# A graph layer with three branches: maxima moved into attention, GpSimd splits, added rows in two transfers, identity turns on TensorE

## The reference, cut to what matters

```
xn = layernorm(x)
# graph branch (gat_conv twice, 4 heads of 192, then 2 heads of 96)
h = (layernorm(xn) * g + b) @ W;  e = leaky_relu(s_src[src] + s_dst[dst], 0.2)
alpha = softmax of e over the edges of each dst;  out = segment_sum(alpha * h[src], dst)
gnn = concat(xn, out2) @ Wu + bu
# mixing branch: random features of k and q, y = (qp @ kptv) / (D + eps), projected
x = x + gnn + mix
# experts: router softmax over 8, top 2, balanced gates, silu(f @ w1) @ w2
x = x + sum over the two chosen of gate * expert(layernorm(x))
```

## Time and profile before

| | us |
|---|---|
| median of 3 runs | 1066.67 |
| lowest, highest | 1063.98, 1069.22 |
| the profiled execution: time | 1061.51 |
| its span | 1059.8 |
| PE busy | 925.7 (87%) |
| DVE busy | 627.1 (59%) |
| ACT busy | 386.2 (36%) |
| POOL busy | 389.6 (37%) |

### The profile page before, as it was taken

One profiled execution on the slowest core, in us unless ns is written; L12 is line 12 of the kernel. 1 busy time (PEld: TensorE's weight loads), 2 busy tenths in 40 slices (PEclk: granted clock), 3 DMA queues, 4 the chain that ended last, 5 costly groups with the idle time before them and its releaser, 6 DMA issues.

```text
span 1059.8 us, 13855 instructions
## 1 busy us (share of the span) xinstructions
PE 925.7 (87%) x5064; PEld 785.8 (74%) x5064; DVE 627.1 (59%) x1222; ACT 386.2 (36%) x575; POOL 389.6 (37%) x302
## 2 busy tenths in 40 slices
PE   3899899999999999999189999897888469999993
PEld 3798785786678899999088988886877457666672
DVE  7676995602078132386989999695996763222221
ACT  2543330223344000244576766346863401121120
POOL 3058888888888874000110000000000313434441
PEclk9999999969999999999589999989988759999997
DMA  9994579333226449600140000216005924666664
GB/s 315 232 161 83 96 203 263 51 45 45 1 1 145 63 92 287 200 2 1 51 149 23 1 1 1 88 63 208 2 1 199 363 60 91 119 120 119 120 120 60
DMA packets 78417, 112.43 MB, mean 106 GB/s; under 512 B 34994, under 2 KB 53933, under 8 KB 78351
## 3 DMA queue, kind: packets, MB, share of 16 engines
q0 software_dynamic: 35264, 39.86, 22.9%
q1 hardware_dynamic: 40781, 65.39, 19.2%
q10 hardware_dynamic: 2306, 6.29, 1.5%
HBM read 80.02 MB, written 31.49 MB: 105 GB/s over the span
## 4 chain that ended last, share of the span: by engine, by line
PE 53%; DVE 20%; DMA 16%; issue 6%; ACT 2%; SPq 1%; POOL 0%; POOLq 0%; DVEq 0%; ACTq 0%
PE bank L1621 41%; DMA out<-orow,send 14%; PE bank L1890 9%; DVE pbuf L1399 4%; DVE pbuf L1373 3%; DVE sb_before L1318 3%; DVE junk_k L1194 2%; PE bank L1632 2%; DVE h L1382 2%; DMA keyrow<-key_d 2%; SPq L552 1%; DVE o L1382 1%; PE bank L1826 0%; DVE sb_stats L1142 0%; DVE xnT_lo L1118 0%
## 5 line engine op out<-in xcount | busy, mean ns | idle before, releaser
L661 POOL DMA_INDIRECT table<-match_n,slot_ix x168 | 276.2, 1644 | 90.2 <-issue 48.9
L1890 PE MATMUL bank<-h,pbuf 128*128 128x197 f32 (+1 forms) x1200 | 194.5, 324 | 29.6 <-DVE pbuf L1399 28.6
L1890 PEld LDWEIGHTS bank<-h,pbuf 128*128 128x128 f32 x1200 | 186.7, 199 | 37.4 <-DVE pbuf L1399 34.2
L1194 DVE SCALAR_TENSOR_TENSOR junk_k<-keyrow,key,sb_before 128x384 uint8<-128x384 f32 x168 | 92.7, 614 | 21.8 <-DMA keyrow<-key_d 11.5
L1318 DVE CUSTOM_DVE_ANT_0 sb_before<-a_row,pen 128x1280 bf16<-128x1280 f32 x60 | 89.4, 1491 | 27.3 <-ACT pen L958 11.2
L1606 DVE TENSOR_SCALAR orow<-bank,gates 128x384 f32<-128x384 f32 x54 | 33.4, 618 | 115.8 <-PE bank L1621 115.8
L692 POOL IOTA cst_i<- 128x128 int32 x1 | 0.2, 229 | 271.8 <-DVE o L1382 271.8
L1016 ACT ACTIVATE pbuf<-pbuf 128x1280 f32<-128x1280 f32 x60 | 76.1, 1269 | 64.4 <-DVE pbuf L1373 64.4
L1399 DVE SCALAR_TENSOR_TENSOR pbuf<-pbuf,cnt 128x1280 f32<-128x1280 f32 x60 | 88.7, 1485 | 0.0
L1621 PE MATMUL bank<-xnT_hi,w_hi 128*128 128x512 f32 (+1 forms) x216 | 85.1, 394 | 3.7 <-DVE xnT_lo L1118 2.8
L728 POOL DMA_INDIRECT out<-orow,send x27 | 42.9, 1587 | 111.5 <-DMA out<-orow,send 92.5
(11 more groups left out here) (346 smaller groups left out, 1668.4 us busy)
## 6 DMA issues: line engine op xcount, KB each, us to landing
keyrow<-key_d SPq DMA_DIRECT2D x28, 384.0 KB
cnt<-table POOLq DMA_DIRECT2D x20, 320.0 KB, 9.3
f_all<-in_w1T SPq DMA_DIRECT2D x8, 768.0 KB, 10.6
f_all<-in_w2T SPq DMA_DIRECT2D x8, 768.0 KB, 12.2
u_row<-m_d POOLq DMA_DIRECT2D x8, 640.0 KB, 6.3
w_raw<-in_kqvT SPq DMA_DIRECT2D x4, 1152.0 KB
acc_d<-ubuf SPq DMA_DIRECT2D x20, 192.0 KB, 2.6
x<-acc_d SPq DMA_DIRECT2D x10, 384.0 KB, 6.1
```

What stands on the lines that cost most here:

```text
L661: pool.indirect_dma_start(table[i], bass.IndirectOffsetOnAxis(ap=slot_ix[:, g:g + 1], axis=0), match_n[:, g:g + 1], None, compute_op=ALU.a ...
L1194: nc.vector.scalar_tensor_tensor(out=junk_k[g % 2][:, :], in0=keyrow[c % KR][:, w:w + KW * P], scalar=key[:, g:g + 1], in1=before[:, first ...
L1890: ins = nc.tensor.matmul(b[:, d * stride:d * stride + v.shape[-1]], score[:, dt * P:(dt + 1) * P], v, start=st == 0 and d == 0, stop=st == ...
```

## The change

Six edits. (1) Masks come in pairs in the second half (`PEN_AT`), the maxima are taken for heads 0 and 1 together, then head 2; those of head 3 for tiles 4 to 9 are taken inside first attention, after steps 2, 5, ... 17, and its row is written by SP straight from `ucol` in 4-byte pieces. The joining of the biases is done after step 1. The row loads of head 0 wait for the maxima of head 2. (2) The subtraction on `cnt` is spread over the last projection tiles. (3) The low part of the last weight half and the low part of the output weight (`wuo_lo`) are made by GpSimd. (4) In the middle `wuT` and `rsum` go ahead of `aR`; ScalarE starts the second attention after head 0's maxima and copies the `uR2` banks of head 1 at steps 2 and 3. (5) Each addition of result rows is two transfers of 384 channels, with a semaphore for each half. (6) TensorE turns the identity 40 times ahead of the first sums and 28 times ahead of the first expert tile.

```
-        PEN_AT = [(0, 2), (0, 4), (0, 7), (0, 8), (1, 0), (1, 1), (1, 2), (1, 3), (1, 4), (1, 5)]
-        ROWS_AT = {(1, 6): 0, (1, 9): 1}
+        PEN_AT = {(0, 2): [0], (0, 3): [1], (0, 4): [2], (0, 6): [3], (1, 0): [4, 5], (1, 1): [6, 7], (1, 2): [8, 9]}
+        ROWS_AT = {(1, 5): 0, (1, 6): 1, (1, 8): 2}
+        LESS_AT = {(1, 3): [0], (1, 4): [1, 2], (1, 5): [3], (1, 6): [4, 5], (1, 7): [6], (1, 8): [7, 8], (1, 9): [9]}
...
+            sp.wait_ge(m_done, H1)
+            sp.dma_start(m_d[2 * (H1 - 1) * NT:2 * H1 * NT, :].rearrange("(k t) p -> p k t", k=2), ucol[:, H1 - 1, :, :],
+                         allow_slow_non_contiguous=True).then_inc(m_out[H1 - 1], 16)
...
+            pool.wait_ge(w_hi_done, SPLITS.index(A0 + 1) + 1)
+            finished(pool, "wb", 1)
+            i, gain = SLOT[A0 + 1], gb_c[:, 0, :].unsqueeze(2).broadcast_to([P, KD, HALF])
+            nc.gpsimd.tensor_tensor(w_raw[i][:, :, :], w_raw[i][:, :, :], gain, ALU.mult).then_inc(gain_done, 1)
+            pool.wait_ge(gain_done, 1)
+            ins = nc.gpsimd.tensor_tensor(w_lo[i][:, :, :], w_raw[i][:, :, :], w_hi[i][:, :, :].bitcast(F32), ALU.subtract)
+            ins.then_inc(w_split, 1)
...
+            pool.wait_ge(g_hi_done, 1)
+            nc.gpsimd.tensor_tensor(wuo_lo[:, :, :], wuo_raw[:, :, :], wuo_hi[:, :, :].bitcast(F32), ALU.subtract).then_inc(g_split, 1)
...
-            def send_rows(a):
+            def send_rows(a, hf):
...
+                    pool.wait_ge(added_out[hf], 16 * a)
+                pool.wait_ge(orow_done, 2 * a + hf + 1)
+                pool.indirect_dma_start(half_rows, bass.IndirectOffsetOnAxis(ap=send[:, hf, a:a + 1], axis=0),
+                                        orow[a % 3][:, hf * HALF:(hf + 1) * HALF], None,
+                                        compute_op=ALU.add, bounds_check=2 * N - 1).then_inc(added_out[hf], 16)
...
-            act.wait_ge(max_done, MAX1 + 2 * NT)
-            attention(H1, H2, u2_row_b, row_ready_2)
+            act.wait_ge(max_done, MAX1 + NT)
+            def rows_between(i):
+                if i in (2, 3):
+                    rows_out("uR2", (i - 2,), 1, (u1_row_b, u2_row_b)[i - 2][1])
...
+            for dt in range(4, NT):
+                evacuated(dve, "pen", dt, 0), evacuated(dve, "pen", dt, 1)
+                masked_max(pen[dt], a_row, (0, 1), dt)
+            dve.wait_ge(max_done, NT)
+            leaky_max(H1, 0, 1), leaky_max(H1, 1, 1)
+            for dt in range(4, NT):
+                if dt == 7:
+                    max_row_out(0), max_row_out(1)
+                masked_max(pen[dt], a_row, (2,), dt)
+            dve.wait_ge(max_done, NT + NT - 4)
+            leaky_max(H1, 2, 1)
+            def between_first(i):
+                if i == 0:
+                    max_row_out(2)
+                if i == 1:
+                    bias_of_layer()
+                if i % 3 == 2 and i < 18:
+                    masked_max(pen[4 + i // 3], a_row, (3,), 4 + i // 3)
+                if i == 18:
+                    dve.wait_ge(max_done, MAX1)
+                    leaky_max(H1, 3, 1)
...
+            def keep_running(name, n):
+                b = take(pe, *name)
+                for _ in range(n):
+                    nc.tensor.transpose(b[:, 0:P], ident[:, :], ident[:, :])
+            keep_running(("agg", 0, 0), 40)
...
+            keep_running(("yT", 0, 0), 28)
             turn_rows(0)
```

More of the change, by code:

```diff
@@ L1016, in attention @@
                     nc.scalar.activation(pbuf[i % 3][:, :], pbuf[i % 3][:, :], ACT.Exp).then_inc(e_done, 1)
-            attention(0, H1, u2_row, row_ready_1)
-            for h in range(H2):
-                rows_out("aR", (), h, a2_row[h])
+                    between(i)
+            attention(0, H1, u2_row, row_ready_1, lambda i: None)
             act.wait_ge(g_in, 16)
@@ L1029, in _ @@
                                          ACT.Copy).then_inc(free("wuT", k, m), 1)
+            nc.scalar.activation(lr[:, NT, :], finished(act, "rsum")[:, 0:EM], ACT.Copy).then_inc(free("rsum"), 1)
+            for h in range(H2):
+                rows_out("aR", (), h, a2_row[h])
             b = finished(act, "wuR")
@@ L1351, in _, with between_second, attention @@
                 nc.vector.tensor_copy(mrow[h % 2][:, :], b[0:2 * NT, 0:P]).then_inc(free("mT", h), 1)
-            def attention(h0, heads, row_ready, u1_r, stride, chans, out_rows, added, stage, nbank, per):
+            for dt in range(4, NT):
[19 more added lines that the diff above has]
+                    leaky_max(H1, 3, 1)
+            def between_second(i):
+                pass
+            def attention(h0, heads, row_ready, u1_r, stride, chans, out_rows, added, stage, nbank, per, between):
                 seq = [(h, st) for h in range(heads) for st in range(NT)]
@@ L1812, in score_columns, with spread_row @@
                 ins.then_inc(full("dot"), 1)
+            def spread_row(stage, k, h, cols):
+                for c, (s, w) in enumerate(CHUNKS):
+                    b = take(pe, stage, *k, h, c)
+                    for t in chunk_tiles(c):
+                        ins = mm(b[:, t * P - s:(t + 1) * P - s], cols[:, t:t + 1].broadcast_to([P, P]), ident[:, :], True, True)
+                    ins.then_inc(full(stage, *k, h, c), 1)
             def max_rows(h):
@@ L1913, in _ @@
             pe.wait_ge(router_in, 16)
+            pe.wait_ge(mean_done, 2)
+            b = take(pe, "rsum")
+            for m in range(KD):
+                ins = mm(b[:, 0:EM], ones[:, :], rw_raw[:, m, :], m == 0, m == KD - 1)
+            ins.then_inc(full("rsum"), 1)
+            pe.wait_ge(dots_done, 2)
+            for h in range(H2):
+                spread_row("aR", (), h, scol[:, h, :])
             evacuated_all(pe, "wuT")
-            pe.wait_ge(mean_done, 2)
             b = take(pe, "wuR")
@@ L1920, in _ @@
             ins.then_inc(full("wuR"), 1)
-            b = take(pe, "rsum")
-            for m in range(KD):
-                ins = mm(b[:, 0:EM], ones[:, :], rw_raw[:, m, :], m == 0, m == KD - 1)
-            ins.then_inc(full("rsum"), 1)
             def spread_shifts(h):
```

133 lines of the change are left out of this document (57 added, 76 removed).

## The result

The changed kernel takes 1037.42 us (median of 4 runs, 1033.1 to 1039.45); the kernel before on the same chip takes 1067.14 (median of 4, 1063.98 to 1069.22). The ratio is 0.9719, 95% interval 0.9679 to 0.9758. On a second chip it was 1036.49 against 1063.83, ratio 0.9735 (0.9705 to 0.9764). The prediction was 1036, range 1027 to 1049.

What follows compares the result with a forecast made beforehand. It took the first gap, first attention, the middle and the experts' chain of adding transfers as what bounds the kernel. Terms summed to -30.7 us: 1061.51 to 1030.8, or 1036 on the median's scale, range 1027 to 1049.

Steps and rivals of the forecast that it cites:

- First gap: Masked maxima to first sum of attention: first sum at 518.5 instead of 534.46, -15.9 us, GpSimd passes charged to VectorE.
- the spread of head 0: Middle: TensorE there at about 705, small group done at 707.2, then 16.2 us of TensorE work to the last spread.
- Forty turns: Ahead of attention's first sums: keep TensorE's clock up; half of the 2.3 us effect credited, -1.2 us.
- What attention pays: First attention: maxima, bias additions, row copy and small group inserted on VectorE lengthen it, +6.9 us (bounds 3 and 11.9).
- Middle: Between the attentions: earlier row copies and maxima, ScalarE starting sooner; first sum at 729.8 against 738.77, -9.0 us.
- Attention 2: Second attention: first two steps at 2.5 us each, -1.8 us; six copies returning at steps 2 and 3, +0.8 us.
- Experts: Expert part: 28 turns -2.4, half-row transfers -4.4 and -3.7 us.
- the first (sends stay the bound): Experts: half lands no sooner, or GpSimd needs 6.6 us a tile; yields about 2 instead of 10.5, 1044.5; chance 0.2.
- The second (no lock): Gap and middle: maxima not locked or passes cheap; gap 2 us better, middle 3, 1031; chance 0.13.
- The fourth: Experts: the two adding transfers run one after the other; slower, 1189 at a period of 12; chance 0.04.
- The fifth: Both sets of turns: they do not do what is said, nothing else fails; 1039.5; chance 0.05.
- the third: Lock worse than charged: 5.9 us passes, TensorE waiting, clock not held, insertions near full price; 1045; chance 0.14.

Runs made afterwards that it cites:

- first profile: Profiled execution of the changed kernel in its first measurement, against the kernel before: 1039.45 us in that execution; median 1037.42 us, ratio 0.9719.
- e0: The changed kernel again, nothing altered, beside the kernel before on a second chip: 1036.49 us, ratio 0.9735.
- e1: Changed kernel with one adding transfer of a whole row per expert tile again, halves undone: 1043.75 us, ratio 0.9818.
- e3b: Repeat on another chip of the changed kernel with both low splits back on VectorE: 1024.57 us, ratio 0.9646.
- e3: Changed kernel with both low splits moved from GpSimd back to VectorE: 1024.99 us, ratio 0.9637.
- e6: Changed kernel with both splits on VectorE and four of head 3's six maxima in VectorE's wait ahead of attention: 1024.52 us, ratio 0.9654.
- e7: Changed kernel with ScalarE's old order ahead of second attention (copies head 1's six banks, waits for all maxima): 1038.44 us, ratio 0.978.
- e10: Changed kernel with 66 instead of 40 turns ahead of the first sums: 1034.18 us, ratio 0.9742.
- second profile: Profile of the unaltered changed kernel run again beside the kernel before on a second chip: median 1036.49 us, ratio 0.9735.
- e5: Changed kernel with head 3's six maxima and their small group ahead of attention again: 1027.4 us, ratio 0.9683.
- e8: Changed kernel with splits on VectorE, four head 3 maxima in its wait, no 40 turns, 8 turns before the second-layer row copies: 1020.58 us, ratio 0.9601.
- e2: Changed kernel without the 40 and the 28 turns: 1038.11 us, ratio 0.9755.
- e4: Kernel before with only the adding transfer split in halves: 1053.96 us, ratio 0.9923.

## Why the prediction was right, and where its steps were not

The time and the direction were right, and so was the mechanism of each large part. Three terms were off by more than a microsecond: the first gap, the spread of head 0 in the middle, and the 40 turns. On the prediction's own ruler the parts sum to about 3 us less than it said: the stretches give -26.3, and the start of the maxima 1.4 us sooner, which it had counted in the gap, -27.7 against -30.7. (ScalarE's copy of the fourth h1 tile starts 0.31 us after the first maximum before, at 445.23, and 1.67 after it now, at 450.80.) The median difference of 29.7 on that chip, 27.3 on the second, holds some scatter of the start besides.

- **First gap, -15.9: measured -14.2.** The lock was sized well: 8.8 us charged, 8.6 measured. Missing are 1.7 us. On the prediction's scale (times less the 5.6 us by which h1's fourth output came later) the maxima of head 2 end at 507.3 and not at 506.6, the row loads are issued 0.5 us behind that where nothing was counted, and from issue to use they take 6.44 us and not 5.95. What the paired masks, the order of heads and the spread count copies each gave of this gap no run separates.
- **Forty turns, -1.2: measured -1.0 in the first profile and 0 in the second.** The credit of one half was an average, and the runs show what it averages: behind 40 turns TensorE rests 3.6 to 3.9 us, and the clock fell in e0, e1 and e3b (attention 1 150.4 to 150.5 us, as without turns), held a moment in the first profile and in e3 (149.5), and held in e6 and e7. Where the clock held (e7, e10) attention 1 is 1.9 us shorter, a little less than the 2.3 of full effect. So the half was luck in the single case and roughly right as an average; in e10, where the turns leave 0.70 us of rest, it held.
- **What attention pays, +6.9: measured +5.2 and +6.2** (first and second profile, clock included). With no half clock at all it is some 6.5, an estimate from e10's 148.6, and from 144.3 before less the 2.2 us that 4.4 us at half clock had cost. e5 isolates the largest item: six maxima and the small group cost 5.3 us, 5.9 by the prediction's own items. What the prediction did not ask is whether the move paid at all. It had VectorE waiting from 506.6 to 514.0 on its own scale, 7.4 us into which four of the six maxima fit; e5 shows that leaving them ahead is better, and e8 against e3b that leaving four there is.
- **Middle, -9.0: measured -7.2.** The step that failed is the spread of head 0. The prediction had TensorE there at about 705 and the small group done at 707.2, and counted nothing for the rest between; TensorE rests 2.86 us, and the spread takes 6.36 us instead of 4.73. The price of the weight difference on VectorE was right (3.0, measured 3.15), but its consequence for the clock was not counted; e3 gives 4.5 us back by undoing it. e7 puts 4.7 of the 7.2 us on ScalarE's early start.
- **Attention 2, -1.8 + 0.8: measured -0.9.** The first sums take their 2.5 us each; the copies at steps 2 and 3 were not looked at by themselves.
- **Experts, -10.5: measured -10.4.** Inside it, the 28 turns bring 1.5 at the first product and not 2.4 (e2). The halves, forecast at 8.1, bring 7.3 by e1 and 7.2 by e4 in the medians, 6.5 and 10.1 in the profiles. The cycle of TensorE without waits is 6.05 us, not the 6.32 that was read from one interval. Sends are 6.2 us apart (864.98 to 1026.52 for the first halves), a little less than the 6.3 to 6.4 forecast. A half lands 4.3 us after its issue (median, e5) and not 4.9; the prediction's lower bound was 4.2. The chain of halves made GpSimd wait 0.8 us in all.

Of the rivals, the first (sends stay the bound) is refuted by the waits of GpSimd, 0.8 us for landings where they were 80.2 in e1, and by the landing after 4.3 us. The second (no lock) is refuted by the rows of 5.20, 6.34 and 4.64 us. The fourth did not happen. The fifth came in part: the 28 turns gave under two thirds of their credit, the 40 nothing in the second profile. Of the third's pieces only the clock not held came; the passes themselves took 3.9 and 5.0 us, not 5.9.

**The lock beside the rows.** The Trainium skill (SBUF — State Buffer, Who interferes with whom) says that the pair of ports that VectorE shares with GpSimd is an exclusive lock, that a VectorE instruction with two inputs in SBUF contends for it with a GpSimd instruction that reads SBUF, and that the order of issue decides who blocks. The custom maximum obeys it in these rows, in both directions. The Trainium skill (GPSIMD Engine Reference, Performance versus the Vector engine) gave an estimate of 5.1 us a pass; measured are 4.78 and 6.30, and without the wait for a running maximum 3.9 (the multiply) and 5.0 (the subtract, which the estimate fits). What the prediction concluded from it, that the work would leave VectorE's list and not its time, is what e3 shows: on VectorE the splits cost 3.3 and 1.8 us, on GpSimd they cost VectorE 8.6 and 3.15.

## What to carry to other kernels

Before moving a VectorE operation to GpSimd, compare what it takes on VectorE with how long VectorE stands still beside it; here the move cost VectorE 11.7 us where it saved 5.0, and put a rest in front of TensorE besides. Work moved off the path to a start belongs first into the wait that its move opens, and only the remainder into the loop behind. Turns that are to keep the clock cannot be counted on while a rest stays behind them (held in two of seven profiles with 3.6 to 3.9 us left), and a chain of dependent transfers is worth splitting as soon as the engine feeding it is faster than one link.

## What the runs showed of the hardware that was not expected

- A rest of 1.17 us ahead of the same 40 instructions left the clock at full speed in seven of ten profiles (4.73 us) and dropped it in three (6.36 us). A 1.6 us difference between two profiles can be this alone. The three are just those in which the clock had not fallen at the first sums of attention 1, some 150 us earlier, so a clock held in one place can be paid for in another; that the one causes the other is not shown.
- GpSimd's issue of an adding transfer takes 1.56 us for half rows and 1.59 us for whole ones: two halves cost twice the issue. But a half lands 4.3 us after it, a whole row 5.5.
- The lock between VectorE and GpSimd works both ways for the custom maximum: beside a pass it ends 1.35 us after the pass, and a pass issued into it starts when it ends (3.34 us from there to its end, whether it was issued 0.70 or 0.29 us before).
- Without any difference in the code ahead of it, the start of the first maximum scatters by 8 us between executions of the changed kernel and its variants. For changes of a few us, stretches between fixed instructions tell more than the total.
